# Two expert loops of a fused network: the two halves of a chunk's sum are added by TensorE products with stacked identities instead of by VectorE

## The reference, cut to what matters

```python
# level 1: d=64, h=128, e=16
h1 = jnp.einsum('bsd,edh->bseh', x, w1)
h2 = jnp.einsum('bsd,edh->bseh', x, w2)
hidden = jax.nn.silu(h1) * h2
expert_out = jnp.einsum('bseh,eho->bseo', hidden, w3)
return jnp.einsum('bseo,bse->bso', expert_out, dispatch)

# level 2: d=64, h=256, e=8
h = jax.nn.gelu(jnp.einsum('end,edh->enh', xe, W1) + b1[:, None, :], approximate=False)
y = jnp.einsum('enh,ehd->end', h, W2) + b2[:, None, :]
out = (weights[:, :, None] * sel).sum(axis=1)      # sel: y of the token's top 2

# around both
t = t + ffn(layernorm(t))
```

## Time and profile before

| | us |
|---|---|
| median of 3 runs | 752.04 |
| lowest, highest | 749.76, 755.81 |
| the profiled execution | 752.59 |
| its span (first to last instruction) | 750.9 |

### The profile page before, as it was taken

One profiled execution on the slowest core, in us unless ns is written; L12 is line 12 of the kernel. 1 busy time (PEld: TensorE's weight loads), 2 busy tenths in 40 slices (PEclk: granted clock), 3 DMA queues, 4 the chain that ended last, 5 costly groups with the idle time before them and its releaser, 6 DMA issues.

```text
span 750.9 us, 11502 instructions
## 1 busy us (share of the span) xinstructions
PE 610.5 (81%) x3354; PEld 395.3 (53%) x3354; DVE 459.8 (61%) x1366; ACT 368.9 (49%) x781; POOL 251.8 (34%) x317
## 2 busy tenths in 40 slices
PE   5778494668999999999957997989999998753762
PEld 3565443556555555555546775974455444432541
DVE  5444888877777777777836584852344334176466
ACT  3233495176534444444425554555666675234545
POOL 6401646160553444344440000532322433051005
PEclk9986696556999999999969997858999999885695
DMA  4800000112543425252210000023322220000001
GB/s 104 150 3 1 2 0 1 28 30 62 114 96 80 113 56 113 57 112 57 56 37 0 1 1 1 7 40 92 84 57 57 82 59 29 1 1 0 2 0 56
DMA packets 24527, 34.55 MB, mean 46 GB/s; under 512 B 10984, under 2 KB 20224, under 8 KB 22368
## 3 DMA queue, kind: packets, MB, share of 16 engines
q1 hardware_dynamic: 24480, 33.95, 19.5%
HBM read 32.50 MB, written 1.44 MB: 45 GB/s over the span
## 4 chain that ended last, share of the span: by engine, by line
PE 61%; DVE 22%; ACT 7%; issue 5%; POOL 4%; ACTq 0%; DMA 0%; DVEq 0%; POOLq 0%
PE ps L1747 13%; PE ps L2332 8%; PE ps L2316 8%; PE ps L1767 6%; DVE ST L485 3%; PE ps L2438 2%; PE ps L602 2%; PE ps L777 2%; PE ps L2686 1%; PE ps L2697 1%; PE ps L1350 1%; PE ps L2047 1%; DVE U L585 1%; ACT act_buf L1713 1%; DVE tok_split L597 1%
## 5 line engine op out<-in xcount | busy, mean ns | idle before, releaser
L1452 POOL TENSOR_TENSOR out_acc<-out_acc,tok_tmp 128x512 f32<-128x512 f32 x80 | 103.4, 1292 | 216.8 <-DVE tok_tmp L1661 117.3
L1747 PE MATMUL ps<-tokT,w 128*128 128x512 f32 x512 | 137.1, 415 | 2.7 <-ACT act_buf L1713 1.3
L1747 PEld LDWEIGHTS ps<-tokT,w 128*128 128x128 f32 x512 | 94.7, 194 | 52.0 <-issue 24.3
L1713 ACT ACTIVATE act_buf<-ps 128x512 f32<-128x512 f32 x128 | 76.0, 597 | 92.0 <-PE ps L1747 89.0
L2316 PE MATMUL ps<-tokT,w 128*128 128x512 f32 x256 | 70.1, 418 | 2.1 <-ACT hid_buf L2294 2.1
L2316 PEld LDWEIGHTS ps<-tokT,w 128*128 128x128 f32 x256 | 47.1, 195 | 30.0 <-ACT hid_buf L2294 14.7
L602 PE MATMUL ps<-ident,tok_split 128*128 128x128 f32 x160 | 33.6, 380 | 30.6 <-DVE tok_split L597 29.5
L1656 DVE TENSOR_TENSOR hid_buf<-act_buf,ps 128x512 f32<-128x512 f32 x64 | 43.5, 685 | 20.2 <-ACT act_buf L1713 16.0
L1656 DVE TENSOR_TENSOR tok_split<-act_buf,ps 128x512 f32<-128x512 f32 x64 | 43.4, 686 | 16.3 <-ACT act_buf L1713 14.6
L505 POOL TENSOR_TENSOR nmean<-mean2x,neghalf 128x8 f32<-128x8 f32 x20 | 5.1, 254 | 133.6 <-DVE var L492 133.5
L530 ACT ACTIVATE U<-X,nmr,rstd 128x64 f32<-128x64 f32 x104 | 36.5, 429 | 23.2 <-POOL nmr L508 18.1
(11 more groups left out here) (473 smaller groups left out, 1147.1 us busy)
## 6 DMA issues: line engine op xcount, KB each, us to landing
disp_all<-disp_dram SPq DMA_DIRECT2D x32, 512.0 KB, 6.2
disp_all<-disp_dram SPq DMA_DIRECT2D x32, 256.0 KB, 3.9
w_raw<-in_L_ffn_w SPq DMA_DIRECT2D x4, 512.0 KB, 7.9
XIN<-in_x SPq DMA_DIRECT2D x4, 256.0 KB, 3.6
w_raw<-in_L_ffn_W SPq DMA_DIRECT2D x2, 512.0 KB, 5.9
out<-XIN SPq DMA_DIRECT2D x4, 256.0 KB, 2.2
fc_raw<-in_L_conv_upfc_w SPq DMA_DIRECT2D x1, 512.0 KB, 4.9
w<-in_L_ffn_w SPq DMA_DIRECT2D x1, 512.0 KB, 10.1
```

Of the source, the lines that this page charges most:

```text
L1452: pool.tensor_tensor(out_acc[:, :], out_acc[:, :], weighed[p % 2], ALU.add).then_inc(mm["acc"].sem, 1)
L1713: act.activation(act_buf[e % 2][:, :], ps[:, e % 2, :], ACT.Silu).then_inc(mm["act"].sem, 1)
L1747: last = pe.matmul(ps[:, 2 * k + e % 2, :], w12[:, part, k, EXPERT1[e], :], tokT[:, bass.ts(i, CHUNK)], start=(part == 0), stop=(part == 1))
```

## The change

The four transposes of a `back` become four plain products of the same `out_acc` blocks (stationary, 128x128) with `ident2` (moving, 64 columns). Since `ident2` is two identities one above the other, a product gives 128 tokens x 64 channels with the two halves already added. VectorE's reduce and `out_sum` are gone; `experts_add` now adds bank 7 of PSUM straight to `X`, in level 1 at expert 7 instead of 8. `back` of chunk i waits for the addition of chunk i-1 (`x`) where it waited for its reduce (`ta`), and so do the first users of the PSUM banks behind each loop.

```diff
-        def experts_sum(dve, mm, i):
+        def experts_add(dve, mm, i):
 
             dve.wait_ge(*mm["t_ps"](i + 2))
-            dve.tensor_reduce(out_sum[:, :, :], ps[:, 7, :].rearrange("p (t h c) -> p t c h", h=2, c=C), X_AXIS,
-                              ALU.add).then_inc(mm["ta"].sem, 1)
-
-        def experts_add(dve, mm, i):
-
-            dve.wait_ge(*mm["ta"](i + 2))
             xs = X[:, bass.ts(i, 4), :]
-            dve.tensor_tensor(xs, xs, out_sum[:, :, :], ALU.add).then_inc(mm["x"].sem, 1)
+            dve.tensor_tensor(xs, xs, ps[:, 7, 0:4 * C].rearrange("p (t c) -> p t c", c=C), ALU.add).then_inc(mm["x"].sem, 1)
...
                         if e == 7:
-                            experts_sum(dve, mm, prev)
-                        if e == 8:
                             experts_add(dve, mm, prev)
                         if e == 9:
                             dve.wait_ge(*mm["x"](prev + 1))
...
             def back(i):
 
                 pe.wait_ge(*mm["acc"](1 + (i + 1) * (PAIRS1 - 1)))
-                pe.wait_ge(*mm["ta"](i + 1))
+                if i >= 1:
+                    pe.wait_ge(*mm["x"](i))
                 for t in range(4):
-                    last = pe.transpose(ps[:, 7, t * P:(t + 1) * P], out_acc[:, t * P:(t + 1) * P], ident[:, :])
+                    last = pe.matmul(ps[:, 7, t * C:(t + 1) * C], out_acc[:, t * P:(t + 1) * P], ident2[:, :], start=True, stop=True)
                 last.then_inc(mm["t_ps"].sem, 1)
...
-            pe.wait_ge(*e1["ta"](NCHUNK + 1))
+            pe.wait_ge(*e1["x"](NCHUNK))
```

More of the change, by code:

```diff
@@ L244, in build @@
         route2 = [route(U[:, :, :], NT, E2)]
-        out_sum = sb("out_sum", [P, 4, C], region="mid")
         wq_raw = sb("wq_raw", [INNER, C])
@@ L1474, in build @@
                      (2 + N1, "act m1"), (4 + NCHUNK * PAIRS1, "o_ps"), (2 + NCHUNK * PAIRS1, "w"),
-                     (1 + NCHUNK * (PAIRS1 - 1), "acc"), (1 + NCHUNK, "t_ps ta"))
+                     (1 + NCHUNK * (PAIRS1 - 1), "acc"), (1 + NCHUNK, "t_ps"))
         e1["o_ps"].lead = 4
@@ L1534, in e1_pool @@
             chunk_rstd(pool, NCHUNK - 1, eps_c, m["d_var"], m["d_rstd"])
-        def experts_sum(dve, mm, i):
+        def experts_add(dve, mm, i):
             dve.wait_ge(*mm["t_ps"](i + 2))
-            dve.tensor_reduce(out_sum[:, :, :], ps[:, 7, :].rearrange("p (t h c) -> p t c h", h=2, c=C), X_AXIS,
-                              ALU.add).then_inc(mm["ta"].sem, 1)
-        def experts_add(dve, mm, i):
-            dve.wait_ge(*mm["ta"](i + 2))
             xs = X[:, bass.ts(i, 4), :]
-            dve.tensor_tensor(xs, xs, out_sum[:, :, :], ALU.add).then_inc(mm["x"].sem, 1)
+            dve.tensor_tensor(xs, xs, ps[:, 7, 0:4 * C].rearrange("p (t c) -> p t c", c=C), ALU.add).then_inc(mm["x"].sem, 1)
         def experts_finish(dve, mm, i):
-            experts_sum(dve, mm, i)
             experts_add(dve, mm, i)
@@ L1642, in e1_vector @@
             dve.sem_inc(mm["w"].sem, 2)
-            dve.sem_inc(mm["ta"].sem, 1)
             router_logits(dve, mm, route1, 0, E1, b_gw[:, :], 6)
@@ L2144, in build @@
                      (4 + NCHUNK * U2, "act"), (NCHUNK * U2, "h_ps"), (2 + NCHUNK * PAIRS2, "o_ps w"),
-                     (1 + NCHUNK * (PAIRS2 - 1), "acc"), (1 + NCHUNK, "t_ps ta"))
+                     (1 + NCHUNK * (PAIRS2 - 1), "acc"), (1 + NCHUNK, "t_ps"))
         e2["o_ps"].lead = 2
@@ L2431, in conv @@
                 elif g == 1:
-                    pe.wait_ge(*e2["ta"](1 + NCHUNK))
+                    pe.wait_ge(*e2["x"](NCHUNK))
                 for t in range(9):
```

## The result

| | before | after |
|---|---|---|
| median, us (4 runs each) | 752.73 | 759.5 |
| lowest, highest | 749.76, 755.81 | 756.36, 766.92 |
| the profiled execution, its span | 752.59, 750.9 | 756.36, 754.6 |

The ratio is 1.0105, with a 95% interval of 1.0053 to 1.0157: the changed kernel is slower by 0.5 to 1.6%. Every ratio in this document is taken over the undisturbed executions of both kernels and is not the quotient of the two medians, which is 1.0090 here. The two profiled executions are only 3.8 us apart, and their stages outside the loops differ too; so the stages have to be compared one by one.

What follows compares the result with a forecast made beforehand. TensorE was taken to bound both loops. Fourteen ways back at 0.45 us more gave +6.3 us, less 0.28 and 0.19 us behind the loops, +5.8 us: a median of 757.8 us, 0.8% slower, range 754.0 to 761.0 us.

Steps and rivals of the forecast that it cites:

- the line of 1%: Whole kernel: slower by over 1% (7.5 us), what measurement can tell from no change; chance 0.24.
- the sum: Whole kernel: 6.3 us added in the loops, less 0.28 and 0.19 us behind them, +5.8 us.
- What bounds the kernel: Both loops: TensorE sets the pace, busy 16.00 of 16.00 us per level 2 chunk, 24.25 of 24.70 in level 1.
- Two pairs per product: Way back, both loops: each plain 4-byte product runs as two load-and-matmul pairs, 8 pairs instead of 4.
- The size of this term: TensorE's way back: four more pairs at 0.112 us, 0.41 to 0.86 us; 14 x 0.45 = +6.3 us.
- the longer lone group of L2130: Level 2's attention: 8 pairs in 1.16 us, giving an upper bound of 0.64 us more per way back.
- The rival of dearer pairs: Ways back in the loops: switching from 512-column streams costs 0.57 to 0.64 us more each, up to 760.5 us; chance 0.18.
- Only the columns count: Ways back in the loops: stay at 0.41 us as loads go ahead, 751.5 us; chance 0.07.
- VectorE's relief: Level 1's loop: less VectorE work costed at 0; as a rival, up to 4.0 us back, 753.8 us; chance 0.06.
- The ends: Behind each loop, where the chain runs through VectorE: -0.19 us for level 1, -0.28 us for level 2.
- the detour: Level 1, once per chunk: chain leaves TensorE through ScalarE, VectorE and GpSimd, 1.0 us of waiting, claimed to stay unchanged.

Runs made afterwards that it cites:

- the early order: Kernel before, with level 1's statistics step 5 at expert 11 instead of 13 and GpSimd's scales ahead of its second addition; ratio 0.9964 (0.9927 to 1.0001).

## Why the prediction was right

**The result** of 759.5 us lies in the range of 754.0 to 761.0 us, 1.7 us over the forecast of 757.8 us. The measured ratio, 1.0105, stands just across the line of 1%, where I had put 0.24; its interval covers both sides. By the stages the change costs 6.9 us, where the sum had 5.8.

**What bounds the kernel** was read rightly: TensorE in both loops. Doubled transposes lengthen both chunks by their own time, and the missing reduce changes neither.

**Two pairs per product** was the step on which all hung, and it held: 64 matmuls for 8 ways back, and with numbers that need one pair the cost of a way back fell to 0.06 us.

**The size of this term** was off. I had 0.45 us for a way back and 6.3 us in all; measured were 0.50 us for the way back, 0.49 to 0.57 us for a chunk and 7.4 us in all. The four additional pairs did cost 4 x 0.112 us. What was left out is the edge of 0.06 us, since I took the start and end of the group over from the transposes, and some 0.07 us per chunk of level 2 of unknown cause. I had set the longer lone group of L2130 aside as the way through the array; the way back after takes 1.10 us for its eight, close to that group's 1.16. The rival of dearer pairs named a cost of this kind, once per switch into small products, but put it at 0.12 to 0.19 us where the edge is 0.06; its 0.57 us and more were not met by the way back, though level 2's chunk comes up to it.

**Only the columns count** is refuted from both sides: 64 and 128 columns take the same 0.91 us. By an estimate from the Trainium skill, "TensorE: Matmul & The Clock Gate", section "Back-to-back issue gap", with its 81 ns per pair of 128 columns, the way back would have been some 0.65 us; the trace has 0.91. The four passes of a true 4-byte product, by the Trainium skill, "FP8 and Floating Point Precision", section "TensorE Precision Notes", agree with a dearer product; the trace shows two pairs of them, and their price goes by pairs, not by columns.

**VectorE's relief** was costed at 0 inside the loops: 24.66 and 16.02 us without the reduce. The reason given, that it meets ScalarE again by expert 10, is in the trace after, with the same 0.03 us. That number was misread as time to spare: it passes between silu and gate in the kernel after too, where VectorE does wait. In the kernel before, the statistics instruction ahead of that gate runs from 314.80 to 315.01 us, right up to the gate's start at 314.99, so VectorE had caught up with nothing left over. The zero held, but narrowly. Of VectorE's busy time 9.3 us went (459.8 to 450.5 us by the page), not 12: in level 2's chunk it is 0.69 us as expected, in level 1's 0.47 us instead of 0.81. There neighbouring instructions overlap, which busy time counts once: the reduce ends at 310.72 + 0.68 = 311.40 us, and the next instruction has begun at 311.32. The range was said to leave out half of this rival; with 754.0 us as its lower end it leaves out next to nothing of it (753.8 us).

**The ends** were foreseen at -0.19 and -0.28 us; they gave -0.25 and -0.29.

## What to carry to other kernels

Where TensorE sets the pace, count a small step on it in pairs of weight load and matmul, not in products or columns: a plain product of 4-byte numbers is two pairs, a transpose of them one, so an addition moved from VectorE, where it cost no time, into a product can double the bill of the step on TensorE. Before work is taken off an engine, look for the next point at which that engine must wait for another anyway: relief ahead of such a point was worth nothing here, and the detour went only when the order of the work on VectorE and GpSimd was changed.

## What the hardware showed that I had not expected

A pair with a 128x128 stationary operand costs 0.11 us from start to start with 64 columns as with 128, plain or transposing, at the upper clock: 0.91 us for eight plain ones with their edge in both widths, 0.85 us for eight transposes.

A weight load takes 0.19 us for a plain or a rounded product and 0.14 us for a transpose of the same 128x128 block.

A two-input VectorE instruction of 128x4 elements from SBUF (`m_between`) took 0.94 us while GpSimd was adding 128x512 blocks, and 0.17 us in the early order, where GpSimd stood idle beside it. In the changed kernel it ends at 319.67 + 0.94 = 320.61 us, 0.02 us after the end of these two additions (317.84 + 2.75):

```profile
317.84 2.75 POOL L1451 TENSOR_TENSOR out_acc<-out_acc,tok_tmp 128x512 f32<-128x512 f32 x2 [4.61 <-DVE tok_tmp L1652]
```

That stretch was part of level 1's detour.
